# Three operations moved one step later in a two-layer model kernel: the low half of O in the attention, the router and the similarity in the combining stage

## The chip, the cores and the metric

The kernel runs on one core of a Trainium2 chip. The metric is the device time of one execution in microseconds (us). The core has five engines that run their own instruction lists in order and meet at semaphores: TensorE (PE in the profile, with its weight loads as PEld), VectorE (DVE), ScalarE (ACT), GpSimd (POOL) and SyncE (SP), which here only issues transfers.

## The reference

The reference is a two-layer model on x of 2 x 2048 tokens with 512 features, all in float32:

```python
x = L0_attn_x
xn = _layernorm(x)
s = _L0_attn_ref(xn, ...)        # 16 heads of 32, window of 128 keys and 16 persistent keys
g = _silu(_L0_ffn_ref(xn, ...))  # 32 experts, 6 of them per token, and a shared MLP of 704
x = x + s * g
xn = _layernorm(x)
s = _L1_attn_ref(xn, ...)        # layer norm, K and V rotated, A = sum over tokens of cos(K)*cos(V)
g = _silu(_L1_ffn_ref(xn, ...))  # shared MLP of 2048, one of 256, weighted by a router's top 2
return x + s * g
```

Two parts of it matter here. The attention of layer 0 is

```python
scores = einsum("bqhd,bkhd->bhqk", q, k) * scale, masked
attn = softmax(scores)
out = einsum("bhqk,bkhd->bqhd", attn, v) @ Wo
```

and between the layers the shared MLP of layer 0 is finished, x + s * g is formed and normed, and from the normed rows come the router's logits of layer 1 (512 to 8), its K and V (512 to 1024), and the similarity A, one number per feature and sequence.

## The kernel before, in words

The 4096 tokens are 32 tiles of 128; four tiles are a group, of which there are 8. The kernel runs in stages, one after the other: norm and projections, routing, attention (`phase_attend`), the 32 experts, the combining stage (`phase_mix`), and the last stage. Each matmul with float32 accuracy is done as three with operands split into a high half and a low half (`mm3`, L105 to L107): the high half is a rounded copy made by ACT, the low half is the difference, made by DVE.

**Attention.** The loop runs over steps s, one for each head of each tile (512), and some 17 more to drain. Every engine has its own copy of that loop with its own list of things to do in a step. `tile_of(s, offset)` gives tile u if s = 16 u + offset, so an offset says how many steps after its first head a tile's operation comes; the offsets around the change are counted from X_AT = 17. In step s

- PE computes the scores of head s + 3 (L877), waits for the exponential of head s, transposes every second step a pair of heads (`turn`, L894), and does for an older tile: the products with V (L907), the transposes of its sums (`turn_sums`), the spread of 1/sum (L935), the persistent values (L923), and in steps X_AT + 11 to X_AT + 14 the projection by Wo, a fourth in each (`project`, L105 to L107 into `a_psXY`). The first of these waits for `o_split`.
- DVE masks the scores of head s + 3 and takes their minimum (`top`, L1037), copies transposed pairs 0, 2, 4, 6 and 7 of a tile out of PSUM (`copy_out`, L1047), and for an older tile: `divide` in step X_AT + 6 (O times 1/sum, L1060), `out_lo` in step X_AT + 7 (the low half of O, L1064, which sets `o_split`), `finish` in step X_AT + 15.
- ACT takes the exponential of head s + 2 (`exps`, L983), copies the other transposed pairs (L992), and makes in step X_AT + 7 the high half of O (`out_hi`, L1010), for which `out_lo` waits.

`top`, `exps` and the scores have three buffers (SR = 3).

**Combining.** Here 18 steps make a group: the shared MLP has 6 blocks of 128, and each block has 3 steps. PE's main work in a step is, by k mod 3: the gate projection of a block (L105 to L107 into `b_psG`, 12 matmuls), its up projection (`b_psU`), the down projection of the block before (`b_psY`). Behind the main work each step does what is due for the one or two groups before, by their step `rel`. For tile j of a group, with XS = 8 and first step XS + 4 j (`tile_at`):

- step 0 of the tile: `turn` transposes its normed rows into the bank `psX` (PE, L1744); ACT copies the high half (`x_upper`, L1872), DVE makes the low half (`x_lower`, L2029) and sets `x_split`.
- step 1: `router` (PE, 12 matmuls of 8 columns into `psL`, a part of the bank `psX`), DVE copies the logits (L2131), which frees the bank for the next `turn`; POOL stores xT.
- step 2 and 3: `keys(t, 0)` and `keys(t, 1)`, 12 matmuls of 512 columns each into `psK` (PE), and DVE's copy with scale and bias (L2041), for which PE waits before it writes the same bank again.
- step 4: ACT squares K and V, POOL rotates and multiplies them into `prod` (L1654 to L1669).

A group as a whole has at rel 2 the sums (DVE, L1978) and gates (ACT, L1855), at rel 3 and 4 the residual (DVE, L1986 to L1990, three operations for each tile), at rel 5 to 7 the statistics, and at rel A_AT = 28 `similar` (PE, 32 matmuls of one column into `psA`, also in the bank `psX`), which must come after the first router of the next group; DVE copies its result at A_AT + 1 (L2142), and the second `turn` of the next group waits for that copy. When PE has no main work left, the last two groups drain.

Of the kernel before, what the change touches and what calls it, by code (L numbers as in the profile page):

```python
# [97 lines left out]
def f(ap):  # L98

    return ap.bitcast(F32)  # L100
# [500 lines left out]
def phase_attend(nc, env):  # L601
# [23 lines left out]
    with ctx:  # L625
# [140 lines left out]
        X_AT = 17  # L766
# [29 lines left out]
        def tile_of(s, offset):  # L796

            u, rest = divmod(s - offset, NH)
            return u if rest == 0 and 0 <= u < TILES else None
# [226 lines left out]
        @block.vector  # L1026
        def _(dve):
            dve.wait_ge(mask_in, 64)

            def top(s):  # L1030
                u = s // NH
                if s >= SR:
                    dve.wait_ge(p_ready, s - SR + 1)
                dve.wait_ge(s_full, s + 1)
                i = u % BT
                m = mask[i if i < 2 else 3 if u % R == 0 else 2]
                dve.tensor_tensor_reduce(out=sm[s % SR][:, :], in0=psS[s % SR][:, PERSIST:2 * KW], in1=m[:, :],  # L1037
                                         scale=-SCALE, scalar=3.0e38, op0=ALU.add, op1=ALU.min,
                                         accum_out=nmax[s % SR][:, :]).then_inc(s_used, 1)

            def copy_out(s):
                u, h = divmod(s, NH)
                p = h // 2
                if h % 2 and p in ON_DVE:
                    slot_free(dve, u, p)
                    dve.wait_ge(pT_full, u * HH + p + 1)
                    dve.tensor_copy(pT[(u * HH + p) % TR][:, :], bank(u, p)[:, :]).then_inc(pT_dve, 1)  # L1047

            def invert(u):
                dve.wait_ge(p_ready, (u + 1) * NH)  # L1050
                if u >= 2:
                    dve.wait_ge(x_full, u - 1)
                dve.reciprocal(rl[u % 2][:, 0:NH], rs[u % 2][:, :]).then_inc(rl_ready, 1)

            def divide(u):
                dve.wait_ge(pers_done, u + 1)
                dve.wait_ge(r_ready, u + 1)
                if u:
                    dve.wait_ge(o_split, u)
                dve.tensor_tensor(o[:, :, :], psO[:, :, :], rb[:, :, :], ALU.mult).then_inc(o_ready, 1)  # L1060

            def out_lo(u):
                dve.wait_ge(o_hi, u + 1)
                dve.tensor_tensor(oT[1][:, :, :], o[:, :, :], f(oT[0][:, :, :]), ALU.subtract)\  # L1064
                   .then_inc(o_split, 1)

            def finish(u):
                if u >= 2:
                    dve.wait_ge(y_out[u % 2], 16 * (u // 2))
                dve.wait_ge(y_full, u + 1)  # L1070
                dve.tensor_copy(y[u % 2][:, :], psXY[:, :]).then_inc(y_ready, 1)

            def find_slots(u, part):

                i8f, eid, pos = place
                if part == 0:
                    dve.tensor_tensor(hits[:, :, :], i8f[:, u, 0:TOPK].unsqueeze(2).to_broadcast([P, TOPK, E]),
                                      eid[:, :].unsqueeze(1).to_broadcast([P, TOPK, E]), ALU.is_equal).then_inc(found, 1)
                elif part == 1:
                    dve.wait_ge(found, 3 * u + 1)  # L1080
                    dve.tensor_tensor(hits[:, :, :], hits[:, :, :], pos[:, u:u + 1, :].to_broadcast([P, TOPK, E]),
                                      ALU.mult).then_inc(found, 1)
                elif part == 2:
                    dve.wait_ge(found, 3 * u + 2)
                    dve.tensor_reduce(slot[:, :], hits[:, :, :], AX.X, ALU.add).then_inc(found, 1)
                else:
                    dve.wait_ge(found, 3 * u + 3)
                    dve.tensor_copy(env.slot_i[:, u, :], slot[:, :]).then_inc(slot_ready, 1)

            dve.wait_ge(wo_hi, 1)  # L1090
            dve.tensor_tensor(wo[1][:, :, :], wraw[:, :, :], f(wo[0][:, :, :]), ALU.subtract).then_inc(wo_split, 1)
            for s in range(SR):
                top(s)
            for s in STEPS:
                if s + SR < N:
                    top(s + SR)
                for part in range(4):
                    if (u := tile_of(s, FIND_AT + 2 * part)) is not None:
                        find_slots(u, part)
                if (u := tile_of(s, X_AT - 3)) is not None:  # L1100
                    invert(u)
                if s < N:
                    copy_out(s)
                if (u := tile_of(s, X_AT + 6)) is not None:
                    divide(u)
                if (u := tile_of(s, X_AT + 7)) is not None:
                    out_lo(u)
                if (u := tile_of(s, X_AT + 15)) is not None:
                    finish(u)
# [368 lines left out]
def phase_mix(nc, env):  # L1478
# [10 lines left out]
    QS = GROUPS * NB  # L1489
    XS = 8  # L1490
    SUM_AT = 2
    A_AT = 28
    with ctx:
        x2 = [env.x0, [sb(f"b_x1{h}", [P, KC, G], F32R) for h in range(2)]]
        wd = [sb(f"b_wd{h}", [P, NB, D], F32R) for h in range(2)]
# [87 lines left out]
        def tile_at(g, rel, first):  # L1583

            j, rest = divmod(rel - first, 4)
            return GT * g + j if rest == 0 and 0 <= j < GT else None
# [116 lines left out]
        def _(pe):  # L1703
# [98 lines left out]
            for g, k, after in steps():  # L1802
                if g is not None and k % 3 < 2:
                    gate_up(g, k // 3, k % 3)
                elif k % 3 == 2 and g is not None and g * NB + k // 3:
                    down_of(g * NB + k // 3 - 1)
                elif k == 2 and g is None and after and after[0] == (GROUPS - 1, 2):
                    down_of(QS - 1)
                if g == 0:
                    for u in FOLD_AT.get(k, ()):  # L1810
                        fold(u)
                for n, rel in after:
                    if (t := tile_at(n, rel, XS)) is not None:
                        turn(t)
                    if (t := tile_at(n, rel, XS + 1)) is not None:
                        router(t)
                    if (t := tile_at(n, rel, XS + 2)) is not None:
                        keys(t, 0)
                    if (t := tile_at(n, rel, XS + 3)) is not None:
                        keys(t, 1)  # L1820
                    if rel == A_AT:
                        similar(n)
# [122 lines left out]
        def _(dve):  # L1945
# [155 lines left out]
            for g, k, after in steps():  # L2101
                if g is not None:
                    m = k // 3
                    q = g * NB + m
                    if k % 3 == 1:
                        product(q)
                        if g == 0 and m + 1 < NB:
                            wd_lower(m + 1)
                    elif k % 3 == 2:
                        h_lower(q)  # L2110
                        if q + 2 < QS:
                            gu_lower(q + 2)
                if g == 0:
                    fold(k)
                for n, rel in after:
                    if rel == SUM_AT:
                        sums(n)
                    if rel in (3, 4):
                        residual(GT * n + 2 * (rel - 3))
                        residual(GT * n + 2 * (rel - 3) + 1)  # L2120
                    if rel == 5:
                        variance(n)
                    if rel == 6:
                        deviation(n)
                    if rel == 7:
                        deviation2(n)
                    if (t := tile_at(n, rel, XS)) is not None:
                        x_lower(t)
                    if (t := tile_at(n, rel, XS + 1)) is not None:
                        dve.wait_ge(l_full, t + 1)  # L2130
                        dve.tensor_copy(env.logits1[:, t, :], psL).then_inc(l_used, 1)  # L2131
                    if (t := tile_at(n, rel, XS + 2)) is not None:
                        keys(t, 0)
                    if (t := tile_at(n, rel, XS + 3)) is not None:
                        keys(t, 1)
                    if rel == 25:
                        norms(n)
                    if rel == 26:
                        over_norms(n)
                    if rel == A_AT + 1:  # L2140
                        dve.wait_ge(a_full, n + 1)
                        dve.tensor_copy(env.aparts[:, n, :], psA).then_inc(a_used, 1)  # L2142

# [549 lines left out]
```

## Time and profile before

| | us |
|---|---|
| median of 3 runs | 4499.61 (4493.49 to 4503.83) |
| the profiled execution | 4502.13 |
| its span, first to last instruction | 4500.4 |
| attention stage, within the span | 386 to 925 |
| combining stage | 2420 to 3175 |
| DVE busy / ACT busy / POOL busy | 2116.4 / 1666.2 / 1353.5 |
| PE busy | 4187.2 (93%) |

Times in the rows are microseconds from the start of the span. A busy PE is one that has a matmul in flight; since matmuls overlap, a row's duration is longer than the distance to the next. PEclk is the clock that TensorE was granted, as a share of full speed; it takes only two values, 2.4 GHz and 1.2 GHz, so a mean of 0.90 is a fifth of the time at the lower one. Idle time in brackets is that of the engine just before the row, with what ended it.

### The profile page before, as it was taken

Reading aid. Unit: us, or ns where it says so; the run is one execution under the profiler, and the core shown is the slowest. Engines: PE = TensorE matmul, PEld = TensorE weight load, DVE = VectorE, ACT = ScalarE, POOL = GpSimd, SP = SyncE. Lnnn points to the kernel's source line nnn. Section 1 sums busy time; section 2 is a strip of 40 time slices with the busy share of each in tenths; the row PEclk is TensorE's granted clock in tenths of the full one; section 3 lists DMA queues with packets and bytes.
Section 4 is the critical chain, followed back from the end, with each engine's and each line's share of the span. In section 5 each row is a group of like instructions: output and inputs, shape, how many; then the busy total and the mean of one; then the engine's idle time right before and its main releaser. Section 6 shows DMA issues by size and latency. Waiting matters only on the chain. (4 is left out here: it accounts for less than half of the span.)

```text
span 4500.4 us, 69429 instructions
## 1 busy us (share of the span) xinstructions
PE 4187.2 (93%) x23045; PEld 3576.7 (79%) x23046; DVE 2116.4 (47%) x4125; ACT 1666.2 (37%) x3234; POOL 1353.5 (30%) x2020
## 2 busy tenths in 40 slices
PE   6975889879999999999997999998899999999998
PEld 5864777779989999989985777776688888788887
DVE  4446777744444444444445444543343333333333
ACT  2214777733434444444433333332232222222222
POOL 0012444445555555555551233334000000000000
PEclk9877999989999999999998999998899999999999
DMA  5767676545556565555645433431422321231321
GB/s 192 280 237 183 127 150 128 113 117 118 133 113 132 119 136 121 129 126 120 135 97 174 155 131 131 155 105 61 147 81 97 99 98 62 100 100 59 102 84 45
DMA packets 351912, 561.41 MB, mean 125 GB/s; under 512 B 33089, under 2 KB 198625, under 8 KB 347490
## 3 DMA queue, kind: packets, MB, share of 16 engines
q1 hardware_dynamic: 282770, 394.19, 29.5%
q0 software_dynamic: 68944, 164.62, 17.1%
q8 instruction: 120, 1.97, 0.2%
q14 instruction: 78, 0.64, 0.1%
HBM read 384.36 MB, written 174.34 MB: 124 GB/s over the span
## 5 line engine op out<-in xcount | busy, mean ns | idle before, releaser
L1250 POOL DMA_INDIRECT acc_d<-e_yw,e_to x208 | 336.0, 1615 | 286.5 <-ACT e_yw L1407 269.9
L2312 POOL DMA_DIRECT2D out<-d_res x32 | 17.3, 542 | 1304.6 <-DVE d_res L2544 1304.6
L2491 DVE TENSOR_TENSOR d_h<-d_sg,d_psU 128x512 f32<-128x512 f32 x144 | 99.0, 687 | 520.3 <-PE d_psU L107 462.0
L983 ACT ACTIVATE a_pr<-a_sm,a_nmax 128x272 f32<-128x272 f32 x512 | 264.4, 517 | 160.3 <-DVE a_nmax L1037 155.7
L105 PE MATMUL e_psG<-e_gu,e_xT 128*128 128x352 f32 x832 | 289.7, 348 | 10.4 <-DVE e_xT L1461 10.2
L1469 DVE TENSOR_TENSOR e_h<-e_sg,e_psU 128x352 f32<-128x352 f32 x208 | 108.3, 521 | 396.0 <-ACT e_sg L1420 393.2
L107 PE MATMUL e_psG<-e_gu,e_xT 128*128 128x352 f32 x832 | 272.4, 327 | 0.0
L106 PE MATMUL e_psG<-e_gu,e_xT 128*128 128x352 f32 x832 | 271.7, 327 | 0.0
L105 PE MATMUL e_psU<-e_gu,e_xT 128*128 128x352 f32 x832 | 271.3, 326 | 0.0
L106 PE MATMUL e_psU<-e_gu,e_xT 128*128 128x352 f32 x832 | 269.9, 324 | 0.0
L105 PE MATMUL e_psY<-e_wd,e_hT 128*128 128x512 f32 (+1 forms) x624 | 265.6, 426 | 1.2 <-DVE e_hT L1452 1.2
L107 PE MATMUL e_psU<-e_gu,e_xT 128*128 128x352 f32 x832 | 266.5, 320 | 0.0
L1220 POOL DMA_INDIRECT e_xs<-xn_d,e_idx x209 | 210.1, 1005 | 174.3 <-POOL e_idx L1217 168.4
L1037 DVE CUSTOM_DVE_ANT_0 a_sm<-a_psS,a_mask 128x272 f32<-128x272 f32 x512 | 216.1, 436 | 95.9 <-PE a_psS L877 61.9
L2419 ACT ACTIVATE d_hT<-d_h 128x512 fp32r<-128x512 f32 x144 | 91.0, 632 | 459.2 <-DVE d_h L2491 401.2
L1420 ACT ACTIVATE e_sg<-e_psG 128x352 f32<-128x352 f32 x208 | 96.4, 463 | 413.5 <-PE e_psU L107 413.5
L107 PE MATMUL e_psY<-e_wd,e_hT 128*128 128x512 f32 (+1 forms) x624 | 247.0, 396 | 0.0
L106 PE MATMUL e_psY<-e_wd,e_hT 128*128 128x512 f32 (+1 forms) x624 | 245.4, 393 | 0.0
L2413 ACT ACTIVATE d_sg<-d_psG 128x512 f32<-128x512 f32 x144 | 86.0, 598 | 422.9 <-PE d_psG L107 422.9
L1401 ACT ACTIVATE e_hT<-e_psH 128x384 fp32r<-128x384 f32 x208 | 102.2, 491 | 370.1 <-PE e_psH L1340 370.1
L105 PE MATMUL d_psG<-d_x,d_gu 128*128 128x512 f32 x576 | 225.2, 391 | 12.8 <-DMA d_x<-xT_d 12.7
L105 PE MATMUL d_psU<-d_x,d_gu 128*128 128x512 f32 x576 | 227.5, 395 | 0.0
(430 smaller groups left out, 12072.7 us busy)
## 6 DMA issues: line engine op xcount, KB each, us to landing
d_gu_raw<-in_wgu SPq DMA_DIRECT2D x144, 512.0 KB, 3.2
qk_d<-f_qk SPq DMA_DIRECT2D x32, 1024.0 KB, 6.6
a_q<-qk_d SPq DMA_DIRECT2D x96, 256.0 KB
a_k<-qk_d SPq DMA_DIRECT2D x96, 256.0 KB, 4.6
e_rawgu<-in_w_gate SPq DMA_DIRECT2D x32, 704.0 KB, 5.9
e_rawgu<-in_w_up SPq DMA_DIRECT2D x32, 704.0 KB, 5.8
b_gu_raw<-in_wgu SPq DMA_DIRECT2D x40, 512.0 KB, 3.9
xT_d<-f_xT SPq DMA_DIRECT2D x16, 1024.0 KB, 14.5
```

What stands on the lines that cost most here:

```text
L105: pe.matmul(out, lhs[0], rhs[1], start=first, stop=False, **kw)
L106: pe.matmul(out, lhs[1], rhs[0], start=False, stop=False, **kw)
L107: return pe.matmul(out, lhs[0], rhs[0], start=False, stop=last, **kw)
L983: act.activation(pr[half][:, h % HH, :], sm[s % SR][:, :], ACT.Exp, bias=nmax[s % SR][:, :], scale=-1.0, accum_out=rs[u % 2][:, h:h + 1]). ...
L1037: dve.tensor_tensor_reduce(out=sm[s % SR][:, :], in0=psS[s % SR][:, PERSIST:2 * KW], in1=m[:, :], scale=-SCALE, scalar=3.0e38, op0=ALU.add ...
L1220: pool.indirect_dma_start(rows[:, :], None, env.xn_d, bass.IndirectOffsetOnAxis(ap=idx[k][:, :].bitcast(U32), axis=0))\
L1250: pool.indirect_dma_start(env.acc_d, bass.IndirectOffsetOnAxis(ap=to[:, :].bitcast(U32), axis=0), yw[:, :], None, compute_op=ALU.add).then ...
L1401: act.activation(hT[0][:, :, :], psH[:, :, :], ACT.Copy).then_inc(hT_hi, 1)
L1420: act.activation(sg[:, :], psG[:, 0:M], ACT.Silu).then_inc(sg_ready, 1)
L1469: dve.tensor_tensor(hv[:, :], sg[:, :], psU[:, 0:M], ALU.mult).then_inc(h_ready, 1)
L2419: act.activation(h2[q % 2][0][:, :], hv[q % 2][:, :], ACT.Copy).then_inc(h_hi, 1)
L2491: ins = dve.tensor_tensor(hv[q % 2][:, :], sg[q % 2][:, :], psU[:, :], ALU.mult)
```

## The change

In the attention, `out_lo` is done in step X_AT + 8 of its tile instead of X_AT + 7, on DVE alone. In the combining stage the router (PE) and the copy of its logits (DVE) are done in the tile's third step, just ahead of `keys(t, 0)`, instead of in its second. `similar` goes from rel 28 to 29, and DVE's copy of its result, which was one step behind it, is now in the same step, 29, so that it stays where it was. No instruction is added or taken away, no tile or semaphore changes.

```diff
@@ phase_attend, block.vector
-                if (u := tile_of(s, X_AT + 7)) is not None:
+                if (u := tile_of(s, X_AT + 8)) is not None:
                     out_lo(u)
@@ phase_mix
-    A_AT = 28
+    A_AT = 29
@@ phase_mix, block.tensor
                     if (t := tile_at(n, rel, XS)) is not None:
                         turn(t)
-                    if (t := tile_at(n, rel, XS + 1)) is not None:
+                    if (t := tile_at(n, rel, XS + 2)) is not None:
                         router(t)
-                    if (t := tile_at(n, rel, XS + 2)) is not None:
                         keys(t, 0)
@@ phase_mix, block.vector
-                    if (t := tile_at(n, rel, XS + 1)) is not None:
+                    if (t := tile_at(n, rel, XS + 2)) is not None:
                         dve.wait_ge(l_full, t + 1)
                         dve.tensor_copy(env.logits1[:, t, :], psL).then_inc(l_used, 1)
-                    if (t := tile_at(n, rel, XS + 2)) is not None:
                         keys(t, 0)
...
-                    if rel == A_AT + 1:
+                    if rel == A_AT:
                         dve.wait_ge(a_full, n + 1)
```

## Rows read from the trace of the kernel before

**Rows 1.** The head of the profile page.
```profile
span 4500.4 us, 69429 instructions
```

**Rows 2.** Windows: stretch, its length, busy us (instructions) by engine, clock, DMA.
```profile
core 0: us, PE busy (x) PEld busy (x) DVE busy (x) ACT busy (x) POOL busy (x), PEclk, DMA share, GB/s
386.00:925.00 539.00, 476.26 (x4576) 399.73 (x4576) 402.41 (x1441) 388.62 (x1217) 239.81 (x389) 0.95 0.62 120
...
2600.00:3060.00 460.00, 449.22 (x2087) 360.48 (x2087) 217.18 (x384) 153.15 (x268) 157.79 (x188) 0.95 0.39 132
```

**Rows 3.** Waits of the attention stage: us in total, times, longest.
```profile
DVE a_oT L1064 <- ACT a_oT L1010: 19.9, 32, 0.7
...
PE a_psXY L105 <- DVE a_oT L1064: 2.2, 1, 2.2
```

**Rows 4.** Timeline of attention, one tile's `out_lo`: start, duration, engine, line [idle before].
```profile
788.65 0.43 DVE L1037 CUSTOM_DVE_ANT_0 a_sm<-a_psS,a_mask 128x272 f32<-128x272 f32 x1
...
789.07 0.62 ACT L1010 ACTIVATE a_oT<-a_o 128x512 fp32r<-128x512 f32 x1
...
789.24 0.38 PE L877 MATMUL a_psS<-a_k,a_q 96*128 96x288 f32 x1 [0.42 <-ACT a_pr L983]
...
789.59 0.51 ACT L983 ACTIVATE a_pr<-a_sm,a_nmax 128x272 f32<-128x272 f32 x1
789.72 0.69 DVE L1064 TENSOR_TENSOR a_oT<-a_o,a_oT 128x512 fp32r<-128x512 f32 x1 [0.63 <-ACT a_oT L1010]
...
790.25 0.66 PE L894 MATMUL a_psP<-ident,a_pr 128*128 128x128 f32 x4 [0.63 <-ACT a_pr L983]
790.33 0.43 DVE L1037 CUSTOM_DVE_ANT_0 a_sm<-a_psS,a_mask 128x272 f32<-128x272 f32 x1
...
790.69 0.68 DVE L1047 COPY a_pT<-a_psP 128x512 f32<-128x512 f32 x1
790.81 0.52 ACT L983 ACTIVATE a_pr<-a_sm,a_nmax 128x272 f32<-128x272 f32 x1 [0.61 <-DVE a_nmax L1037]
...
791.29 0.43 DVE L1037 CUSTOM_DVE_ANT_0 a_sm<-a_psS,a_mask 128x272 f32<-128x272 f32 x1
...
791.48 0.50 PE L105 MATMUL a_psXY<-a_wo,a_oT 128*128 128x512 f32 x1 [0.25 <-ACT a_pr L983]
```

**Rows 5.** Windows: two tiles of attention, and a stretch of combining.
```profile
699.36:715.18 15.82, 14.16 (x144) 11.86 (x143) 12.49 (x46) 12.12 (x40) 6.71 (x12) 1.00 0.74 134
...
746.80:764.10 17.30, 15.63 (x144) 13.22 (x143) 12.49 (x46) 12.23 (x40) 8.12 (x13) 0.90 0.62 123
...
2488.44:2494.01 5.57, 5.57 (x24) 4.69 (x25) 0.17 (x1) 0.46 (x1) 1.08 (x2) 0.73 0.59 204
```

**Rows 6.** Waits of the combining stage from 2482 to 3060.
```profile
PE c_psX L105 <- DVE c_xT L2029: 14.8, 13, 2.1
...
DVE b_h L1966 <- issue: 13.1, 6, 3.5
```

**Rows 7.** Timeline of combining: the router waits, and a group's last tile.
```profile
2488.44 0.27 PE L105 MATMUL c_psX<-c_wr,c_xT 128*128 128x8 f32 x1 [2.15 <-DVE c_xT L2029]
...
2542.83 0.47 PE L105 MATMUL b_psG<-b_x,b_gu 128*128 128x512 f32 x1
...
2547.47 0.27 PE L105 MATMUL c_psX<-c_wr,c_xT 128*128 128x8 f32 x1 [1.64 <-DVE c_xT L2029]
...
2551.43 0.15 DVE L2131 COPY logits<-c_psX 128x8 f32<-128x8 f32 x1
...
2553.52 0.69 DVE L1966 TENSOR_TENSOR b_h<-b_sg,b_psU 128x512 f32<-128x512 f32 x1 [1.94 <-issue]
...
2558.23 0.73 DVE L2041 SCALAR_TENSOR_TENSOR c_kv<-c_psK,stat,bkv 128x512 f32<-128x512 f32 x1
...
2559.02 0.50 PE L105 MATMUL c_psK<-wkv,c_xT 128*128 128x512 f32 x1
...
2573.94 0.27 PE L105 MATMUL c_psX<-c_wr,c_xT 128*128 128x8 f32 x1 [0.46 <-DVE c_xT L2029]
```

**Rows 8.** Timeline of the drain of combining: a wait between the halves of `keys`.
```profile
3132.89 0.50 PE L105 MATMUL c_psK<-wkv,c_xT 128*128 128x512 f32 x1 [0.84 <-DVE c_kv L2041]
```

## What the change will do to the time

> **What bounds the kernel now.** I began with the busy times of each stage, taken from the windows view, and then read who waits for whom inside the two stages that the change touches. One core runs, so there is no other core to compare with. The execution that was profiled has a span of 4500.4 us [rows 1] and took 4502.13 us; the median of the runs is 4499.61 us, 2.5 us less, well inside their own spread of 10 us.
>
> In the attention stage no engine is full: of 539 us, PE is busy for 476, DVE for 402 and ACT for 389 [rows 2]. What sets the pace there is a ring. For each head PE makes the scores, DVE masks them and finds their minimum (`top`), ACT takes the exponential (`exps`), and PE may go on only when the exponential is there. A delay at any link moves everything behind it. In the combining stage, from 2600 to 3060, PE is busy for 449 of 460 us [rows 2]: PE sets the pace, and each microsecond it waits is a microsecond of the kernel, unless another engine would be late anyway.
>
> The waits of the attention stage show DVE standing idle before `out_lo` in all 32 tiles, 19.9 us together, for the ACT copy that makes the high half; PE waited for `out_lo`'s own result only once, for 2.2 us [rows 3].
>
> **Part 1: `out_lo` one step later.** No instruction is added or removed; one subtraction per tile changes its place in DVE's order. Rows 4 show one tile. Heads are counted from 0 in the tile that is running. DVE starts the masking of head 11 at 788.65 and could go on with head 12 about 0.36 us later (that is the distance at which maskings follow one another when nothing holds them: 790.33 to the copy at 790.69), because its scores are long there. Instead it stands still for 0.63 us until ACT's copy at 789.07 ends, does `out_lo` at 789.72, and masks head 12 at 790.33. ACT then finds nothing to do for 0.61 us and takes exponential 12 only at 790.81, and PE, which waits for that exponential, starts the first matmul of the projection at 791.48, 0.67 us behind it [rows 4].
>
> After the change DVE's order is masking 12 at 789.01, the copy of the transposed pair at 789.37, `out_lo` 0.60 us later at 789.97, and it ends at 790.66. ACT takes exponential 11 at 789.59 as before, and exponential 12 right behind it, 0.51 us later (the duration in its row), at 790.10 instead of 790.81: **0.71 us earlier**. The projection could start 0.67 us after that, at 790.77; it needs `out_lo`, which ended at 790.66. So that wait is missed by only about 0.1 us. All later links hang on exponential 12 or 13. The masking of head 13 now begins at 790.58 instead of 791.29, again 0.71 us earlier. The step is repeated in tiles 0 to 30 (for the last tile no masking is queued behind it): 31 x 0.71 = **22.0 us**. The bounds are 0 (projection late by as much as was won) and 31 x 0.71 = 22; I take the upper end, because each link above has its own row. POOL and the queues of SP are not passed by the step: `out_lo` issues no DMA.
>
> **The clock in attention.** From one tile's `sums_out` to the next's there are 31 intervals; 19 last 15.8 to 16.0 us, and 12 last 16.9 to 17.3 us at a mean granted clock of 0.90 [rows 5], which show one of either kind. The clock falls from 2.4 to 1.2 GHz for a short stretch in these tiles, which begins with the projection, directly after PE has waited three times in little more than two microseconds: 0.42 us, 0.63 us, and once more before the projection, 0.25 us [rows 4]. One such fall costs 17.30 - 15.82, about 1.48 us [rows 5]; twelve cost 17.8. The change takes away the third wait and leaves the first two. No row shows what the clock does after 1.05 us of waits instead of 1.30. The nearest rows are in the combining stage: a wait of 0.46 us before the router is never followed by a fall (6 times), one of 1.64 or 2.15 us nearly always (6 of 7; the third row of rows 5 is the stretch behind the first of them, at a granted clock of 0.73). The bounds are +28 us (the clock falls in the 19 other tiles too) and -17.8 us (never again). Ten of the twelve falls gone, **14.8 us**, is my value: falls already come in only 12 of 31 tiles with the waits as they are, so the waits lie near the edge and the change moves them to the good side.
>
> The Trainium skill, "TensorE: Matmul & The Clock Gate", Part 4 (PE-mode transpose), says that transposes do not count as a busy PE in the way that matmuls do. By that the transposes at 790.25, which stand between the waits and the projection, would be part of the quiet time, the clock would fall as often as now, and this term would be 0 instead of 14.8. No row here separates transposes from waits.
>
> **Part 2: the router one step later.** In the combining stage a tile's normed rows are transposed (`turn`), ACT and DVE split them (`x_upper`, `x_lower`), and PE multiplies them by the router weights. With one step of other work between, PE reaches the router before `x_lower` is done: 13 waits, 14.8 us up to 3060 [rows 6]. They are of three kinds [rows 7], which show one of each: 2.15 us once at the very first tile, 1.64 us six times at the last tile of a group (there DVE adds four sums and ACT makes four gates ahead of the split), and 0.46 us six times at the first tile of a group. With two steps between, PE has another twelve matmuls, 2.8 us of work, in front of the router (`psG` begins at 2542.83 and the wait at 2547.47 - 1.64 = 2545.83, less the tail of `turn`). That covers all three kinds. But what is late next?
>
> For the last tile of a group it is DVE. Before it can make `keys` of that tile, which PE awaits before it starts the second half of them, it has `x_lower`, six vector operations for the residual, one product `b_h`, and six more. In rows 7 DVE is done with the first six and the logits at 2551.58, stands idle for 1.94 us until the product starts at 2553.52 because PE is late with `psU`, and starts `keys` at 2558.23; PE begins the second half at 2559.02, directly after. So PE was on DVE's heels already, and the 1.64 us does not come back as such: what comes back is DVE's idle time before the product, since PE will have `psU` ready 1.64 us earlier and without the fall of the clock that follows the wait. That idle time is a row of its own: 13.1 us in 6 times, longest 3.5 [rows 6]. A new wait of about 1.5 us on `kv` takes the place of the old one. The gain: **13.1 us** for the six, 6 x 0.46 = **2.8 us** for the first tiles, and for the very first 2.15 us and the fall behind it, (1 - 0.73) x 5.57 = 1.5 us [rows 5, 7]: **3.7 us**. Together 19.6 us. Bounds: 6.5 (nothing of the six), and 14.8 + 6 falls of 1.5 us = 24 us, if DVE were no limit.
>
> The logits' copy moves behind the product in DVE's order. Only the next `turn` waits for it, two steps on; the store of `xT` on POOL stays where it is, and POOL issues the same DMAs. The wait of DVE for the router is shorter than the one for `keys` directly behind it. Zero, because DVE would wait there anyway.
>
> **Part 3: `similar` one step later.** 32 small matmuls move from before to behind the second half of the keys. They wait for products that POOL ended long before; POOL's next write of `prod` comes after some 4.7 us of other work on that tile. In the drain the change loses the cover of one 0.84 us wait before the second half [rows 8], and a wait of `turn` on the copy of `aparts` gets shorter, since that copy no longer queues behind `keys` on DVE. The one costs 0.84 us and the other gives back up to as much: I take 0. The four router waits of the drain itself stay, because there no other PE work lies between `turn` and the router.
>
> **The sum.** 22.0 + 14.8 + 19.6 = 56.4 us. The profiled execution would come to 4502.1 - 56.4 = 4445.7, the median to 4499.6 - 56.4 = **4443 us**.
>
> **The rivals.**
> - *The clock keeps falling as often.* 22.0 + 19.6 = 41.6: 4458 us. For it: two of three waits stay, and the page above. Chance 0.25.
> - *The clock falls in every tile.* A shorter tile may bring the waits into a worse rhythm: 41.6 - 28 = 13.6: 4486 us. Against it: less waiting than before. Chance 0.08.
> - *The wait moves from DVE to the projection.* `out_lo` ends 0.1 us before PE asks for it. If the copy ahead of it is late, nothing is won in attention: 19.6 alone, 4480 us. Chance 0.08.
> - *Slower, by the same mechanism further on.* PE's order has scores and transposes queued behind the projection. If `out_lo` came 0.65 us later than the projection starts today, 31 x 0.65 = 20 us would be lost, as much as the router wins; that is the point from which it decides. The longer quiet time would also let the clock fall in the 19 other tiles, 28 us: 4499.6 - 19.6 + 20 + 28 = 4528 us. It needs `out_lo` 1.5 us later than worked out. Chance 0.04.
> - *The change doesn't do what it says*: the waits go, and others (`kv`, `aparts`, clock falls behind the new `kv` wait, 6 x 1.5 us) take their place in both stages, within 9 us of before. Chance 0.05.
>
> **How the numbers follow.** The forecast has 0.50: 4430 to 4455, the spread of its clock term and of 3 us between executions. The range reaches over the rivals at 4458 and 4480: 4430 to 4480. It leaves out the falls in every tile, slower, and no change, together 0.17, and a little below 4430. What a measurement of this kernel can tell from no change is about 0.2%, 9 us. Faster by more than that: 0.91; within: 0.05; slower: 0.04.
>
> **What would show it.** Right: DVE's 19.9 us before `out_lo` is gone and ACT's wait for the minimum is down by about 20 us; tiles last 15.1 us, and few have a granted clock of 0.90; no router wait before 3000; a wait of PE of about 1.5 us on `kv` once a group, and the idle time before `b_h` near zero. Wrong: a PE wait on `out_lo` in each tile, tiles of 15.8 us, or granted clocks of 0.9 in most tiles.

## The result, and the profile after

The changed kernel takes 4431.91 us (median of 4 runs, 4428.8 to 4445.42); the kernel before, with the runs made beside it, 4496.55. The ratio is **0.9861**, with a 95% interval of 0.9841 to 0.9882. It is faster: by the ratio 62 us of 4500, and the two medians lie 65 us apart, where 56 were forecast; 4443 us was 11 us too high, inside the range. The execution that was profiled took 4445.42 us; its forecast was 4445.7. Each step of the sum can be looked up in it.

The head of the page, where [rows 1] had 4500.4:

```profile
span 4443.7 us, 69429 instructions
```

**Attention.** The waits from 400 to 869 no longer have a row for `out_lo` behind ACT, which was 19.9 us in [rows 3]. The first view below is that of line 1064: what DVE's idle time before it ended on, and who waited for it (us, times). What is left lies in the drain, where no head stands between the two. The second is a row of the stage's waits: us in total, times, longest. ACT's wait for the minimum was 114.0 us, 249 times, in the same stretch of the kernel before (400 to 911), so it fell by 35 us; about 20 were forecast.

```profile
  ACT a_oT L1010: 0.7, 1
...
  PE a_psXY L105: 2.2, 1
```

```profile
ACT a_pr L983 <- DVE a_nmax L1037: 79.4, 213, 0.9
```

The timeline of one tile, where [rows 4] showed the same operations:

```profile
755.81 0.43 DVE L1037 CUSTOM_DVE_ANT_0 a_sm<-a_psS,a_mask 128x272 f32<-128x272 f32 x1
756.16 0.43 DVE L1037 CUSTOM_DVE_ANT_0 a_sm<-a_psS,a_mask 128x272 f32<-128x272 f32 x1
...
756.39 0.39 PE L877 MATMUL a_psS<-a_k,a_q 96*128 96x288 f32 x1 [0.42 <-ACT a_pr L983]
...
756.53 0.68 DVE L1047 COPY a_pT<-a_psP 128x512 f32<-128x512 f32 x1
756.74 0.51 ACT L983 ACTIVATE a_pr<-a_sm,a_nmax 128x272 f32<-128x272 f32 x1
...
757.13 0.68 DVE L1064 TENSOR_TENSOR a_oT<-a_o,a_oT 128x512 fp32r<-128x512 f32 x1
757.25 0.51 ACT L983 ACTIVATE a_pr<-a_sm,a_nmax 128x272 f32<-128x272 f32 x1
757.40 0.66 PE L894 MATMUL a_psP<-ident,a_pr 128*128 128x128 f32 x4 [0.62 <-ACT a_pr L983]
...
758.02 0.39 PE L105 MATMUL a_psXY<-a_wo,a_oT 128*128 128x512 f32 x1
```

The masking of head 12 follows that of head 11 after 0.35 us instead of 1.68; exponential 12 comes 1.44 us behind the masking of head 11, against 2.16 before, so 0.72 us earlier. `out_lo` ends at 757.81 and the projection starts at 758.02: it is not held up. The 0.25 us of PE idle time ahead of it is gone; the two waits before it, 0.42 and 0.62 us, are not.

Windows from one tile's `sums_out` (ACT's copy of the transposed sums, L998) to the next's, as in [rows 5]: all 31 have a granted clock of 1.00.

```profile
core 0: us, PE busy (x) PEld busy (x) DVE busy (x) ACT busy (x) POOL busy (x), PEclk, DMA share, GB/s
672.89:688.00 15.11, 13.69 (x144) 11.78 (x143) 12.42 (x46) 12.02 (x41) 7.41 (x13) 1.00 0.77 141
...
733.44:748.53 15.09, 13.65 (x144) 11.78 (x143) 12.51 (x46) 12.02 (x41) 7.43 (x13) 1.00 0.73 142
```

**Combining.** The waits from 2446 to 3001 have no router wait any more ([rows 6]: 13, 14.8 us) and none of DVE ahead of `b_h` with the releaser "issue" (6, 13.1 us). In their place stands one wait a group, on the copy of the keys:

```profile
PE c_psK L105 <- DVE c_kv L2040: 9.4, 6, 1.6
```

and in the timeline of a group's last tile, to be laid beside [rows 7]:

```profile
2510.70 0.67 DVE L1965 TENSOR_TENSOR b_h<-b_sg,b_psU 128x512 f32<-128x512 f32 x1
...
2515.39 0.15 DVE L2130 COPY logits<-c_psX 128x8 f32<-128x8 f32 x1
2515.46 0.74 DVE L2040 SCALAR_TENSOR_TENSOR c_kv<-c_psK,stat,bkv 128x512 f32<-128x512 f32 x1
...
2516.25 0.50 PE L105 MATMUL c_psK<-wkv,c_xT 128*128 128x512 f32 x1 [1.56 <-DVE c_kv L2040]
```

DVE goes through its chain without a stop, and PE waits for the end of it.

More came back here than waiting. The two windows below are the stretches of the two wait views, the kernel before first:

```profile
2482.00:3060.00 578.00, 562.06 (x2605) 451.53 (x2606) 268.99 (x476) 194.40 (x340) 195.73 (x233) 0.95 0.39 133
...
2446.00:3001.00 555.00, 545.36 (x2607) 442.99 (x2608) 269.42 (x476) 193.91 (x339) 195.63 (x233) 0.97 0.40 138
```

In the trace TensorE is at 1.2 GHz for 58 us in the first of them and for 31 us in the second: the six half-speed stretches behind router waits are gone, 27 us in all. A stretch at half the clock costs half of its length when PE sets the pace (an estimate), so the clock gives 14 us, and the waits of PE, 15.7 us before and 10.1 us now, give 6.

The stages, measured between fixed operations of each trace (last `sums_out`, first `fold`, last matmul of `similar`), in us:

| | before | changed |
|---|---|---|
| up to the first `sums_out` | 401.9 | 401.4 |
| attention, 31 intervals | 507.6 | 466.7 |
| rest of attention, experts | 1517.9 | 1524.1 |
| combining | 743.6 | 721.4 |
| last stage | 1329.4 | 1330.1 |

40.9 and 22.2 us are won in the two stages, and 6.2 us are lost between the last `sums_out` and the first `fold`, almost all of which is the expert stage, which the change doesn't touch.

### The profile page after: what moved, and what is told of

Same layout as the page of the kernel before. It is cut to its first block and busy times, and to the rows that moved or that the text cites. A ratio compares the mean times of both kernels' runs of the same rounds, so it can differ in the third digit from the quotient of the medians.

```text
span 4443.7 us, 69429 instructions
## 1 busy us (share of the span) xinstructions
PE 4139.1 (93%) x23045; PEld 3550.2 (80%) x23046; DVE 2115.4 (48%) x4125; ACT 1662.0 (37%) x3234; POOL 1352.3 (30%) x2020
## 3 DMA queue, kind: packets, MB, share of 16 engines
q0 software_dynamic: 68944, 164.62, 17.3%
## 5 line engine op out<-in xcount | busy, mean ns | idle before, releaser
L2310 POOL DMA_DIRECT2D out<-d_res x32 | 17.3, 542 | 1305.3 <-DVE d_res L2542 1305.3
```

## The experiments

**The changed kernel once more.** No edit.

> The changed kernel once more, as the measure for the others and for a second profile. If the 6 us that the expert stage was longer in the first profile (1524.1 against 1517.8 us) come from the change (transfers that land in another order), the stage is 1524 us again and the time near 4445. If they are chance of one execution, the expert stage may be anything from 1510 to 1525 us and the time is 4430 to 4445. In both cases attention has 31 intervals near 15.1 us with a granted clock of 1.00.

Measured: 4439.01 us, ratio 0.9864 (0.9841 to 0.9887). Attention 466.8 us, experts 1520.3, combining 721.6. The expert stage does not repeat: over the profiles of this study it lasted 1512 to 1524 us, with no order that follows the edits. The 6 us are chance. Nor does the combining stage, although these two profiles agree to 0.2 us: over the six profiles that have its changed code and `similar` at rel 29 it lasted 714.1 to 721.6 us, and over the four with its code of before 736.6 to 743.6 us. A single pair of profiles therefore tells its gain to some 7 us only; the means are 718.2 and 741.5 us. Attention with `out_lo` at X_AT + 8 lasted 466.7 to 469.1 us in five profiles.

**The attention part alone.**

```diff
-                if (u := tile_of(s, X_AT + 7)) is not None:
+                if (u := tile_of(s, X_AT + 8)) is not None:
                     out_lo(u)
```

> Only out_lo goes one step later. Theory (ring and clock): the ring gives 22 us and the falls of the clock that no longer come give 18 to 20, so 40 to 42 us less than before, ratio 0.991, with tiles of 15.1 us. Rival (the ring alone is out_lo's doing, and the falls went because the rest of the kernel shifted): 22 us, ratio 0.995, tiles of 15.1 and 16.6 us.

Measured: 4455.09 us, ratio 0.9909 (0.9886 to 0.9932): 41 us of 4502. Attention lasted 467.6 us, and all 31 intervals had a granted clock of 1.00. The theory holds: ring and clock both hang on this one line. (The combining stage, which is that of the kernel before, lasted 736.6 us here, 7 us less than there.)

**The combining part alone.** The diff of the changed kernel without the line above.

> Only the router and the similarity go one step later. Theory: DVE's idle time before b_h and the short waits come back, 20 to 22 us, ratio 0.9953; the attention stage is as before, with 12 or so long intervals of 17.3 us. Rival (the router's waits come back whole, with the falls behind them): 24 us or more. Other rival (the new wait on kv eats them): under 10 us.

Measured: 4475.08 us, ratio 0.9951 (0.9936 to 0.9965): 22 us. The interval, 16 to 29 us, rules out the rival of under 10 us; it doesn't separate the theory from the rival of 24 us or more. The trace does: the wait on the keys is there, 9.3 us in six times, so the router's waits did not come back whole. The stage itself lasted 714.6 us. 0.9909 x 0.9951 = 0.9860, the ratio of the whole change: the parts add up. In its attention stage, which is that of the kernel before, 20 of 31 intervals had a granted clock of 0.90, and the stage lasted 519.5 us instead of 507.6. Two of its windows:

```profile
641.34:658.60 17.26, 15.58 (x144) 13.20 (x143) 12.50 (x46) 12.26 (x41) 7.82 (x13) 0.90 0.78 167
658.60:674.42 15.82, 14.16 (x144) 11.86 (x143) 12.49 (x46) 12.15 (x40) 7.13 (x13) 1.00 0.80 180
```

**The kernel before, profiled again.** No edit.

> The kernel before, profiled a second time. In the run with the combining part alone, whose attention stage is that of the kernel before, 20 intervals were long (16.9 to 17.3 us at a granted clock of 0.90), and in the first profile of the kernel before 12. Theory: how many tiles the clock falls in is chance of the execution, so this one has anything from 8 to 22, and the attention stage lasts 507 us plus or minus 12. Rival: the number belongs to the kernel: 12 again.

Measured: 4512.87 us in one run. Attention lasted 520.1 us. Counted with the last interval, which is shorter than the others, the clock fell behind the three waits in 17 of 31 intervals; in the first profile, counted so, in 13, and in the run above in 20. So the number of falls in the same attention code belongs to the execution and not to the kernel. The first profile of the kernel before, from which the clock's term was worked out, was the one with the fewest.

Four more intervals here lasted 17.2 to 17.3 us at a granted clock of 1.00. In each of them ACT stood idle for 1.4 us before `sums_out`:

```profile
520.93 0.49 ACT L998 ACTIVATE a_xT<-a_psP 128x384 f32<-128x384 f32 x1 [1.44 <-remote]
```

PE's transposes of the sums had ended 0.35 us before ACT fell idle, and in the first profile ACT waits here only at the last tile. What held it is not shown. It made some 5 of the 12.5 us by which this stage is longer than the first profile's; five more falls (one of them at another place) made the rest, 7.4 us.

**The wait filled.** In the kernel before, the transposes of heads 10 and 11 are done twice, to the same place:

```diff
-                for hh in (h - 1, h):
+                for hh in (h - 1, h) * (2 if p == 5 else 1):
                     for c in range(2):
```

> The kernel before, with the four transposes of the pair of heads 10 and 11 done twice, into the same place: PE has some more transposes where it stood waiting before the projection, and nothing moves in the ring of scores, minimum and exponential. Theory (the clock falls because PE is quiet too long before the projection, and transposes count as work): the intervals stay at 15.8 us and the long ones of 17.3 us go, 15 to 18 us less, ratio 0.9963. Rival (transposes do not count as work, as the Trainium skill says on the page TensorE: Matmul & The Clock Gate, PE-mode transpose, or quiet time is not the cause): the long intervals stay, ratio 1.000; if the copies hold PE up, up to 32 x 0.2 = 7 us more.

Measured: 4484.26 us, ratio 0.9958 (0.9944 to 0.9971): 18 us less, with more work. Attention lasted 492.2 us, and none of the 31 intervals had a granted clock under 1.00. The ring is as slow as before:

```profile
496.58:512.37 15.79, 14.37 (x147) 12.28 (x147) 12.48 (x46) 12.16 (x39) 7.38 (x13) 1.00 0.71 135
512.37:528.18 15.81, 14.38 (x148) 12.27 (x147) 12.58 (x46) 12.14 (x39) 7.41 (x13) 1.00 0.72 136
```

This separates the two parts of the attention gain, which the change itself can't: here the clock alone was mended, and attention lasted 492.2 us against 507.6, 520.1 and 519.5 us with 13, 17 and 20 falls. Most tiles still last 15.8 us; eight end on the ACT idle time before `sums_out` that the section above showed, 0.6 us each. Of the remaining 25 us down to 467 the ring is 22. It also decides the point that the prediction left open. By the Trainium skill ("TensorE: Matmul & The Clock Gate", Part 4) transposes do not count as a busy PE in the way that matmuls do. The measurement says otherwise and decides: four more of them, in place of the third wait, left the first two waits as they were, 0.42 and 0.62 us, and the clock stayed at 2.4 GHz in every tile.

**The wait filled in the changed kernel.** The same edit on the changed kernel.

> The changed kernel with the four transposes of the pair of heads 10 and 11 done twice, as in the run that filled the wait of the kernel before. Theory: what the filling brought there (17 us) was the falls of the clock; the changed kernel has none left in attention, so that it brings nothing here or costs up to 31 x 0.25 = 8 us, because PE no longer waits at that place: 4435 to 4447. Rival: the transposes help in another way, again some 17 us: 4420.

Measured: 4461.96 us, ratio 0.9893 (0.9861 to 0.9924). By the ratios that is some 14 us slower than the changed kernel (0.9861 and 0.9864), with intervals that overlap. The stage is clearer: attention lasted 495.5 us, 29 us longer, and its combining stage happened to be 7 us shorter. The filling brings nothing where no fall is left, which the theory said; but in attention it costs over three times what was expected. Most tiles last 16.2 to 16.3 us instead of 15.1:

```profile
624.84:641.10 16.26, 14.07 (x148) 12.31 (x147) 12.50 (x46) 11.95 (x39) 7.80 (x14) 1.00 0.83 176
```

The eight transposes take 1.09 us instead of 0.66 for four, and PE begins the projection 0.44 us later behind `out_hi` than in the changed kernel (medians 2.24 and 1.80 us). That much is the filling on the ring; in the kernel before the same instructions stood in a wait and cost nothing. The rest of the 1.15 us a tile stands in one place, ACT's idle time before `sums_out`, by the view of what ended it (us, times):

```profile
  PE a_psP L917: 25.8, 28
```

It is 1.0 to 1.1 us in most tiles, and PE's transposes of the sums, which the view names, had ended 0.35 us before it began. In the changed kernel the same view has 2.1 us, once, at the last tile.

**`out_lo` one step too late.** X_AT + 9 in place of X_AT + 8.

> out_lo two steps later than before (X_AT + 9). Theory: DVE then does it behind the masking of head 13, it ends at 791.02 in the clock of rows 4 instead of 790.66, so the projection starts 0.3 us later than in the changed kernel: tiles of 15.4 us instead of 15.1, attention 9 us longer; no falls of the clock or few: 4440 to 4450. Rival (any place behind the wait is as good, the ring hides it): tiles of 15.1 us.

Measured: 4456.75 us, ratio 0.9895 (0.9878 to 0.9912), attention 487.5 us, all granted clocks 1.00. The direction was right, the size was not: tiles of 15.8 us instead of 15.4. The projection begins 2.09 us behind the start of `out_hi` (median), 0.29 us later than in the changed kernel, just as was worked out. The rows are of one of the few tiles where all of it shows as idle time of PE (elsewhere that is 0.13 us),

```profile
726.23 0.69 DVE L1064 TENSOR_TENSOR a_oT<-a_o,a_oT 128x512 fp32r<-128x512 f32 x1
...
727.07 0.47 PE L105 MATMUL a_psXY<-a_wo,a_oT 128*128 128x512 f32 x1 [0.30 <-issue]
...
733.30 0.49 ACT L998 ACTIVATE a_xT<-a_psP 128x384 f32<-128x384 f32 x1 [0.52 <-PE a_psP L917]
```

and another 0.4 us of the tile is lost at the last row, `sums_out`. The changed kernel has no idle time there:

```profile
763.63 0.47 ACT L998 ACTIVATE a_xT<-a_psP 128x384 f32<-128x384 f32 x1
```

The transposes of the sums still end 0.29 us later than in the changed kernel (7.44 us behind `out_hi` against 7.15, medians), but `sums_out` starts 1.06 us later, behind 0.6 to 0.7 us of ACT idle time in nearly every tile. So in this run and the one before, 0.29 and 0.44 us on the ring cost 0.72 and 1.15 us a tile, and the excess is this idle time. What released ACT the profile doesn't show: the PE work that it names had been done. Neither the forecast nor the expectations had a term for it.

**`out_lo` far too late.** X_AT + 11, the step of the projection's first part.

> out_lo four steps later than before (X_AT + 11), in the step of the first projection. This is the rival that would have made the change slower, brought about on purpose: PE waits for out_lo with scores and transposes queued behind. Theory: the projection starts 1.4 us later than in the changed kernel, tiles of 16.5 us, and with over two microseconds of waits ahead of it the clock falls in most tiles (1.5 us each): attention 510 to 555 us, slower than the kernel before's 508 to 520 or near it. Rival (the clock does not go by the waits): no tile at a mean granted clock of 0.90, attention 510.

Measured: 4541.18 us, ratio **1.0077** (1.0061 to 1.0093), slower than before; attention 582.8 us. The timeline and three windows:

```profile
734.11 0.69 DVE L1064 TENSOR_TENSOR a_oT<-a_o,a_oT 128x512 fp32r<-128x512 f32 x1
...
734.94 0.52 PE L105 MATMUL a_psXY<-a_wo,a_oT 128*128 128x512 f32 x1 [1.35 <-issue]
735.26 0.63 PE L106 MATMUL a_psXY<-a_wo,a_oT 128*128 128x512 f32 x1
```

```profile
402.75:423.47 20.72, 17.33 (x138) 15.08 (x138) 11.38 (x42) 11.83 (x38) 6.83 (x11) 0.75 0.48 90
423.47:441.63 18.16, 15.39 (x144) 13.19 (x143) 12.50 (x46) 12.04 (x39) 7.46 (x12) 0.91 0.62 117
441.63:461.04 19.41, 16.64 (x144) 14.21 (x143) 12.56 (x46) 12.04 (x41) 7.43 (x12) 0.82 0.56 109
```

PE waits 1.35 us, and the second matmul behind it already takes 0.63 us instead of 0.39: 1.2 GHz. The clock fell in all 31 intervals, for 3.4 us in every other one (18.2 us, 0.91) and for 6.8 us in those between (19.4 us, 0.82); the first interval has both. Without its fall the first kind of tile would be 18.16 - 0.09 x 18.16 = 16.5 us, as expected; this is an estimate. My expectation erred in the length of the falls: it had one per tile at 1.5 us, and every other one was twice as long. This is the rival on the slower side, and it exists. With two more steps than in the run before, `out_lo` makes the kernel slower; where between X_AT + 9 and X_AT + 11 the point lies was not measured.

**The similarity back at rel 28.** The changed kernel with

```diff
-    A_AT = 29
+    A_AT = 28
...
-                    if rel == A_AT:
+                    if rel == A_AT + 1:
                         dve.wait_ge(a_full, n + 1)
```

> The changed kernel with the similarity back at rel 28 and DVE's copy of it one step behind; the router stays one step later. Theory: moving the similarity is worth nothing, the combining stage is 715 to 722 us as with it, time as the changed kernel's, 4430 to 4440, ratio to the kernel before 0.986. Rival: it keeps the small matmuls away from the router's, so that without it the clock falls more often, once more in each of seven groups, 10 us.

Measured: 4440.53 us, ratio 0.9856 (0.984 to 0.9872); combining 718.8 us, within the 714.1 to 721.6 us that the stage has with `similar` at rel 29. Nothing that can be measured hangs on this part. The one fall of the clock in this run's attention stage lies at 404.0 us, 1.3 us behind the first `sums_out`, and not behind the waits at `out_lo`.

**The keys first.** The changed kernel, with DVE serving the older group first in one step of 18:

```diff
-                for n, rel in after:
+                for n, rel in (after[::-1] if k == 4 else after):
```

> The changed kernel, and in step 4 of a group DVE serves the older group before the newer: the logits and keys(t, 0) of the last tile come before the second half of the newer group's residual instead of behind it. Theory (DVE's chain is what PE waits for after the change, 1.56 us six times): those waits go, 9 us less than the changed kernel, ratio to the kernel before 0.984. Rival (the residual is late in its place, and the turn of the next group waits for its normed rows): the waits reappear before turn, nothing gained.

Measured: 4416.16 us, ratio **0.9811** (0.9795 to 0.9827), 24 us less than the run of the section above. Combining lasted 699.4 us, below every other profile of the stage (714.1 us and more). DVE now does the keys behind the product, with a short wait of its own, and the second half of the residual after them:

```profile
2590.55 0.67 DVE L1965 TENSOR_TENSOR b_h<-b_sg,b_psU 128x512 f32<-128x512 f32 x1
2591.13 0.16 DVE L2130 COPY logits<-c_psX 128x8 f32<-128x8 f32 x1
2591.81 0.75 DVE L2040 SCALAR_TENSOR_TENSOR c_kv<-c_psK,stat,bkv 128x512 f32<-128x512 f32 x1 [0.52 <-PE c_psK L107]
2592.48 0.68 DVE L1985 TENSOR_TENSOR c_s<-c_s,c_acc 128x512 f32<-128x512 f32 x1
```

PE is never idle in a group: in both windows below its busy time is the whole window. The first two lines are the changed kernel, the last two this one, from one group's first `turn` to the next's:

```profile
2527.35:2615.12 87.77, 86.21 (x410) 70.11 (x408) 43.23 (x77) 30.24 (x54) 31.24 (x37) 0.96 0.41 141
2615.12:2701.31 86.19, 84.62 (x410) 68.73 (x409) 43.29 (x76) 30.26 (x54) 31.24 (x37) 0.98 0.42 144
```

```profile
2519.38:2605.33 85.95, 85.95 (x409) 70.26 (x408) 43.25 (x78) 30.29 (x54) 31.29 (x38) 0.96 0.41 143
2605.33:2688.11 82.78, 82.78 (x409) 67.61 (x408) 43.24 (x78) 30.28 (x54) 31.33 (x39) 1.00 0.43 152
```

So DVE's chain was indeed what PE waited for, and the rival (normed rows too late) is out. The gain of the stage, 22 us against the changed kernel and 19 against the run above, is twice what the six waits of 1.56 us can give. Most of the rest stands in the clock column: the stretch behind `similar`, where the changed kernel's clock falls in every group (0.96, 0.98), is spared in every second group here (1.00). That is 31 us at 1.2 GHz in six groups there and 14 us here, some 8 us of time. Of the seven profiles with the router's new place and the old order on DVE, six had the fall in all six groups and one in five. Why it is spared in every second group was not tried.

## Why the prediction was right

**Part 1, the ring.** Forecast 0.71 us a tile and tiles of 15.1 us; measured 0.72 and 15.1. This was the mechanism as forecast. The order of DVE's five operations, and the 0.1 us by which `out_lo` comes ahead of the projection (0.21 in the trace), were as worked out. The rival in which the wait moves to the projection is real, but one step further on (`out_lo` at X_AT + 9). What no term covered is that ACT can fall idle before `sums_out` when the ring is shifted by a few tenths; at the chosen place it did so in none to three tiles of a profile, 0.6 us each but for one of 1.4.

**The clock in attention** is the term that was mis-sized. I took 14.8 us: ten of twelve falls gone. There were thirteen: the last interval, 16.0 us at a granted clock of 0.89, had been counted among those without a fall. In that pair of profiles all went, and 40.9 - 22 = 18.9 us is close to 13 x 1.48 = 19.2. The rival that falls keep coming is out, and so is the one of a fall in every tile. Other executions of the kernel before had more to lose: with 17 and 20 falls its attention lasted 520.1 and 519.5 us. A single profile gave the price of a fall well (1.48 us) and their number badly. That removing the third wait would remove the falls was a guess at an edge, with no row for two waits alone, and it came out stronger than guessed. In the pair of profiles the 4 us more here and the 2.6 us more in combining were cancelled by the 6 us of chance in the expert stage: that the profiled execution hit the forecast to 0.3 us is luck. Why the changed kernel's three other executions took 4429 to 4432 us, 13 us and more below the profiled one, is not shown, since they were timed and not profiled. Falls in attention can't be it, for the profiled one has none; their mean granted clock over the whole span was 0.965 to 0.966 against 0.963, so some of it lies in the clock of other stages.

**Part 2, the router.** Forecast 19.6 us with DVE's chain as the new limit and a wait of about 1.5 us on `kv`; measured 22.2 us in the profiles, within the 7 us by which the stage varies, and 0.9951, 22 us, by the run of that part alone; the wait is 1.56 us, six times. The clock is in this term too: by that estimate, of the 19 us that the six groups won, 14 are the six half-speed stretches behind router waits and under 6 are waits. The idle time before `b_h` came back as forecast, the router's waits did not come back whole. The keys-first run confirms the limit by taking it away.

**Part 3, the similarity.** Forecast 0, measured 0 within the resolution. In the drain (from 3001 us on in both traces) the waits before the second half of the keys went from 4.2 us in five times to 5.8 in six, the router's from 12.3 to 11.8, and the wait of `turn` on the copy of `aparts` from 1.00 to 0.35 us.

**The slower rival** named the right mechanism: with `out_lo` ending 1.6 us later than worked out the kernel is slower than before. 4528 us had been put on it, and 4541 were measured; the falls that were twice as long are the term that it lacked. That 1.5 us is the point at which it turns was not tested.

## What to carry to other kernels

An operation that waits in an in-order engine costs what is queued behind it; move it behind those neighbours that are ready, and count out the new order to the tenth of a microsecond, since one step too far gave back half the attention gain here and three steps too far made the kernel slower. Count out the other engines' places round the ring as well: most of what the one step cost stood at an ACT operation 6 us behind the move. When a wait of the engine that sets the pace goes, look for the chain that arrives next: its own idle time, and not the length of the wait, is what comes back. And count falls of TensorE's clock in more than one execution before a sum rests on their number.

## What the runs showed of the hardware

- TensorE's clock fell from 2.4 to 1.2 GHz in some tiles and not in others at the same place of the same code: in 13, 17 and 20 of 31 tiles in three executions, each time at a cost of about 1.5 us. It did so about three waits of PE of 0.42, 0.63 and 0.25 us; with the first two alone it never fell there (31 tiles in each of five profiles with `out_lo` at X_AT + 8); with a third of 1.35 us it fell in every tile.
- Four more transposes in place of the last of these waits kept the clock up in 31 of 31 tiles.
- The clock also falls without any wait: behind the 32 matmuls of one column (`similar`) it was at 1.2 GHz for 3.4 or 6.8 us in each of six groups of the changed kernel, with no idle time of PE over 0.15 us in the 9 us before.
- ACT stood idle for 0.3 to 1.4 us before its copy of the sums in some executions and orders and not in others, after the work that the profile names as its releaser had been done; what held it is open.
- The expert stage lasted 1512 to 1524 us in executions of the same code, and the combining stage 714 to 722 us: each as much as a change of 0.2% moves.
